# A fused recurrent attention and feed-forward block on one core: another place for the last projections of a step, and new orders on the engines beside TensorE

## The reference

```python
rkv = einsum('blh,hu->blu', inputs, W_rkv) + b_rkv
r, k, v = split(rkv, 3, axis=-1)
r, k = sigmoid(r), exp(k)
kv = k * v
# y[t] = lam * y[t-1] + u[t], along the tokens, for u = kv and u = k
u1, u2 = scan(lam, kv), scan(lam, k)
a = (u1 + gamma * kv) / (u2 + gamma * k + 1e-06) * r
x = layernorm(inputs + a @ W_o + b_o)

xr = mu_r * x + (1 - mu_r) * x_prev      # x_prev: the token before
xk = mu_k * x + (1 - mu_k) * x_prev
out = sigmoid(xr @ W_r) * (square(relu(xk @ W_k)) @ W_v)
result = layernorm(x + out)
```

## Time and profile before

| | us |
|---|---|
| median of 3 runs | 2535.43 |
| lowest and highest | 2534.3 and 2537.21 |
| the profiled execution | 2535.74 |
| its span (first to last instruction) | 2533.9 |
| TensorE busy in it | 2510.5 |
| VectorE, ScalarE, GpSimd busy | 2013.6, 1267.5, 1245.6 |

### The profile page before, as it was taken

One profiled execution on the slowest core, in us unless ns is written; L12 is line 12 of the kernel. 1 busy time (PEld: TensorE's weight loads), 2 busy tenths in 40 slices (PEclk: granted clock), 3 DMA queues, 4 the chain that ended last, 5 costly groups with the idle time before them and its releaser, 6 DMA issues.

```text
span 2533.9 us, 32904 instructions
## 1 busy us (share of the span) xinstructions
PE 2510.5 (99%) x11268; PEld 2076.7 (82%) x11268; DVE 2013.6 (79%) x2693; ACT 1267.5 (50%) x2157; POOL 1245.6 (49%) x1128
## 2 busy tenths in 40 slices
PE   7999999999999999999999999999999999999998
PEld 6888888888888888888888888888888888888877
DVE  7877888778787787887788777878777888787885
ACT  4545455444554444554545544455444555454545
POOL 6654454445454544535445444444444453545545
PEclk8999999999999999999999999999999999999999
DMA  4001110111100111111111011111111111110100
GB/s 170 26 34 51 45 39 34 34 51 50 34 34 34 51 51 34 46 38 35 51 39 45 34 35 50 50 34 34 35 50 50 34 43 34 43 51 34 51 25 34
DMA packets 57784, 110.63 MB, mean 44 GB/s; under 512 B 7040, under 2 KB 7040, under 8 KB 57088
## 3 DMA queue, kind: packets, MB, share of 16 engines
q1 hardware_dynamic: 57600, 108.31, 12.6%
HBM read 74.73 MB, written 33.55 MB: 43 GB/s over the span
## 4 chain that ended last, share of the span: by engine, by line
PE 98%; ACT 1%; POOL 0%; DVE 0%; DMA 0%; issue 0%; POOLq 0%; SPq 0%; DVEq 0%; ACTq 0%
PE bankA L1086 14%; PE bankA L1088 14%; PE bankA L1087 14%; PE bankB L1102 14%; PE bankB L1104 13%; PE bankB L1103 13%; PE bankB L1147 4%; PE bankB L1148 4%; PE bankB L1146 4%; PE bankB L1124 2%; PE bankA L1102 0%; PE bankA L1104 0%; PE bankA L1103 0%; POOL x_lo L408 0%; DMA wrkv_f<-in_w_rkv 0%; PE bankA L1148 0%
## 5 line engine op out<-in xcount | busy, mean ns | idle before, releaser
L1086 PE MATMUL bankA<-x_hi,wrkv_hi 128*128 128x512 f32 x1488 | 583.9, 392 | 4.7 <-POOL x_lo L408 4.7
L1088 PE MATMUL bankA<-x_hi,wrkv_lo 128*128 128x512 f32 x1488 | 580.5, 390 | 0.0
L1087 PE MATMUL bankA<-x_lo,wrkv_hi 128*128 128x512 f32 x1488 | 580.4, 390 | 0.0
L882 DVE RECIPROCAL gate<-gate 128x512 f32<-128x512 f32 x128 | 429.2, 3353 | 4.4
L413 POOL TENSOR_TENSOR att_f<-att_f,gate 128x512 f32<-128x512 f32 x128 | 209.4, 1636 | 280.1 <-DVE att_f L895 280.1
L1086 PEld LDWEIGHTS bankA<-x_hi,wrkv_hi 128*128 128x128 f32 x1488 | 280.3, 188 | 63.8 <-POOL x_lo L408 5.8
L1088 PEld LDWEIGHTS bankA<-x_hi,wrkv_lo 128*128 128x128 f32 x1488 | 280.1, 188 | 58.7
L1087 PEld LDWEIGHTS bankA<-x_lo,wrkv_hi 128*128 128x128 f32 x1488 | 280.4, 188 | 57.2
L424 POOL TENSOR_TENSOR ve<-mv,eps_ln 128x2 f32<-128x2 f32 x128 | 66.4, 519 | 462.6 <-DVE mv L907 459.6
L440 POOL TENSOR_TENSOR xk_lo<-xk_f,xk_hi 128x512 fp32r<-128x512 f32 x124 | 169.4, 1397 | 244.9 <-ACT xk_hi L667 244.9
L445 POOL TENSOR_TENSOR xr_lo<-xr_f,xr_hi 128x1024 fp32r<-128x1024 f32 x63 | 176.4, 2800 | 202.7 <-ACT xr_hi L672 202.7
(11 more groups left out here) (150 smaller groups left out, 5588.5 us busy)
## 6 DMA issues: line engine op xcount, KB each, us to landing
y<-in_x SPq DMA_DIRECT2D x128, 256.0 KB, 2.7
x_f<-in_xT SPq DMA_DIRECT2D x124, 256.0 KB, 4.0
out<-z SPq DMA_DIRECT2D x124, 256.0 KB, 2.1
wrkv_f<-in_w_rkv SPq DMA_DIRECT2D x3, 768.0 KB, 7.7
xk_f<-in_xT SPq DMA_DIRECT2D x4, 256.0 KB, 4.5
wo_f<-in_w_o SPq DMA_DIRECT2D x1, 1024.0 KB, 11.2
wk_f<-in_w_k SPq DMA_DIRECT2D x1, 1024.0 KB, 13.1
wr_f<-in_w_r SPq DMA_DIRECT2D x1, 1024.0 KB, 15.2
```

The costliest lines, as they stand in the source:

```text
L882: dve.reciprocal(gate[:, c % 2], gate[:, c % 2]).then_inc(rec_made, 1)
L1086: pe.matmul(bank[:], w_hi, hi[:, h], start=(h == 0), stop=False)
L1087: pe.matmul(bank[:], w_hi, lo[:, h], start=False, stop=False)
L1088: last = pe.matmul(bank[:], w_lo, hi[:, h], start=False, stop=(h == NC - 1))
```

## The change

On TensorE, within a step, the projections number (2,1), (3,1) and (3,2) are each issued one place earlier among the work of the older block: project(2,1) ahead of the transposes, project(3,1) ahead of the keys, and project(3,2) ahead of the first half of the receptance, so that between the two halves of the receptance only the first half of the values is left. Nothing is added or taken away. The other three engines get a new order for the same work.

The core of the diff:

```diff
 GpSimd, step
                 att(s, 1)
-                att_low(s, 0)
                 mixed_gate_low(s1, 0)
                 if s1.first():
                     weight_low(W_V, 3)
+                att_low(s, 0)
+                att_low(s, 1)
                 att(s, 2)
                 mixed_gate_low(s1, 1)
-                att_low(s, 1)
                 residual(s1, 0)
 ScalarE, step
                 exp_key(s, 0)
+                exp_gate(s, 0)
                 exp_key(s, 1)
-                exp_gate(s, 0)
                 if s2.exists():
                     normalise_result(s2, 1)
                 normalise_sum(s1, 0)
+                exp_gate(s, 1)
                 normalise_sum(s1, 1)
-                exp_gate(s, 1)
+                exp_key(s, 2)
                 copy_zT(s1)
                 previous_keys(s1)
                 mixed_keys_high(s1)
-                exp_key(s, 2)
                 exp_gate(s, 2)
                 previous_gate(s1, 0)
                 mixed_gate_high(s1, 0)
+                exp_key(s, 3)
                 att_high(s, 0)
-                exp_key(s, 3)
+                att_high(s, 1)
...
                 previous_gate(s1, 1)
-                exp_gate(s, 3)
                 mixed_gate_high(s1, 1)
                 tanh(s1, 0)
-                att_high(s, 1)
-                att_high(s, 2)
+                exp_gate(s, 3)
                 x_high(s.back(-1), 0)
                 x_high(s.back(-1), 1)
                 x_high(s.back(-1), 2)
+                att_high(s, 2)
                 x_high(s.back(-1), 3)
+                normalise_result(s1, 0)
+                tanh(s1, 1)
                 last_column(s1)
-                tanh(s1, 1)
-                normalise_result(s1, 0)
                 att_high(s, 3)
 VectorE, step
+                begin_sum(s1, 0)
                 if s2.exists():
                     gated_values(s2, 1)
-                begin_sum(s1, 0)
                 begin_sum(s1, 1)
-                denominator(s, 0)
                 if s2.exists():
                     statistics(s2, 1, 1, result_rows, y2_made)
+                denominator(s, 0)
...
                 denominator(s, 1)
+                numerator(s, 1)
                 mix_keys(s1)
                 mix_gate(s1, 0)
-                numerator(s, 1)
                 denominator(s, 2)
...
                 gated_values(s1, 0)
+                x_low(s.back(-1), 0)
                 statistics(s1, 1, 0, result_rows, y2_made)
-                x_low(s.back(-1), 0)
                 x_low(s.back(-1), 1)
 TensorE, step
                 project(s, 2, 0)
+                project(s, 2, 1)
                 transposes(s1)
-                project(s, 2, 1)
                 project(s, 2, 2)
                 project(s, 3, 0)
+                project(s, 3, 1)
                 keys(s1)
-                project(s, 3, 1)
+                project(s, 3, 2)
                 receptance(s1, 0)
-                project(s, 3, 2)
                 values(s1, 0)
                 receptance(s1, 1)
                 values(s1, 1)
```

## The result

The changed kernel takes 2555.73 us (median of 4 runs, 2554.55 to 2556.59), the kernel before 2534.86 (4 runs, 2533.66 to 2537.21). The ratio is 1.0081, with a 95% interval from 1.0063 to 1.0098: slower by 0.8%. The forecast was 2557, with a range of 2552 to 2573. The profiled execution of the changed kernel took 2556.59 us, 20.85 more than that of before; its span is 2554.8, 20.9 more than the 2533.9 of the earlier trace rows.

A forecast was written before the change was run, and what follows sets the result against it. TensorE bounds the kernel; `xr_lo` 0.59 us late plus 0.24 start loses 0.83 per step against 0.11 before, so 0.72 over 30 steps adds 21.6 to 2535.74, giving 2557.3 us, range 2552 to 2573.

The forecast's parts named there:

- The bound and the place: TensorE, busy 2510.5 of 2533.9 us, bounds; the loss is a wait for `xr_lo` before the second receptance half.
- the signs named beforehand: In the profile: 30 `xr_lo` waits of 0.7 to 0.9 us, about 22 us more idle, 78.8 us step, chain through L445, L672, L644, L935.
- The chain from E: From the end of the receptance's first half (E), refill, mix, `xr_hi` and subtraction make `xr_lo` at E + 5.87, due E + 5.28.
- The subtraction: GpSimd's L445 making `xr_lo` takes 2.40 us, chosen with 2.37 the shortest and 2.81 as the other end.
- Rival 1: GpSimd's subtraction is disturbed by VectorE's L879 and stays at 2.81 us: 12.3 us more, 2569.6 us; chance 0.15.
- The start behind the release: TensorE, standing idle before the second receptance half, starts 0.24 us behind `xr_lo`, against 0.16 when barely waiting; 0.83 lost per step.
- The values: First half of the values, 0.3 us late for VectorE's L941, costs nothing on top, being part of the 0.83.
- Rival 2: Second half of the values, or next block's `x_lo`, makes TensorE wait; gated tile's margin some 0.25 us; 2566 to 2587; chance 0.14.
- The other moves: Transposes, keys, moved projections, numerator and `att_low` in their new places together cost 0, bounds -1 and +3 us.
- Rivals 3 and 4: 3: chain of 5.28 us or less removes the 0.11 stall, 2532.4 us, chance 0.05; 4: pauses lower TensorE's clock, 2600 or more, 0.02.

The follow-up runs named there:

- experiment 3: Changed kernel with GpSimd's `xr_lo` made in four one-chunk instructions and TensorE waiting for each chunk where first needed: 2541.51 us, ratio 1.0025.
- experiment 4: Changed kernel with ScalarE's two tanh of the first half put ahead of the copy `xr_hi` of the second half: 2562.95 us (one run).
- experiment 2: Kernel before with only project(3,2) moved ahead of the first half of the receptance, all other engines in old order: 2595.91 us (one run).
- experiment 8: Changed kernel with `xr_lo` in four pieces awaited singly, and the values waiting for each chunk of VectorE's L941: 2534.29 us, ratio 0.9998 to before.
- experiment 7: Changed kernel with GpSimd's att_low(s, 1) put back right behind the second `xr_lo` instead of ahead of it: 2576.41 us (one run).
- Experiment 5: Changed kernel with TensorE's whole step in its old order, the other three engines keeping their new orders: 2551.41 us, ratio 1.0065.
- experiment 1: Changed kernel with project(3,2) put back between the first half of the receptance and the first half of the values: 2562.89 us, ratio 1.0110.
- experiment 6: Kernel before with ScalarE's gate exponential of chunk 3 put behind the copy `xr_hi` of the second half: 2531.04 us, ratio 0.9984 to before.

## Why the prediction was right, and where it was not

**The bound and the place.** Right. TensorE has no slack, no instruction was added, and the loss is standing still at the seam between values and second receptance. Experiment 3 takes that wait away and 14 us with it; experiment 4 lengthens its chain by 0.30 and pays for all of it. Of the signs named beforehand, the step of 78.8 us and the chain through L445, L672, L935 and L644 are there; the waits are shorter than the 0.7 to 0.9 us foreseen (0.6 at most in the steps, as the weight load's wait), and the page shows 8.6 us more idle time and not 22, because a part of each stop counts as busy.

**The chain from E.** Right to 0.04 us: mix ended at E + 2.33 (forecast 2.32), `xr_hi` at 3.42 (3.40), GpSimd started at 3.50 (3.47), `xr_lo` made at 5.91 (5.87), 30 times.

**The subtraction.** Right: 2.41 us where 2.40 was chosen between 2.37 and 2.81. Rival 1 is dead for the reason given against it: ScalarE's L612 makes the gate ready at 1071.40, long after GpSimd has begun at 1069.26, and L879 starts at 1072.25, behind the end of L445 at 1071.67. The neighbouring statement, that L445 would be 2.8 in every second instance, was wrong. With the new orders the first halves meet no longer either; GpSimd's L445, all instances, with shortest, median and longest in ns:

```profile
L445 POOL TENSOR_TENSOR xr_lo<-xr_f,xr_hi x63: 2371/2403/2415, 105.4 to 2518.7; 128x1024 fp32r<-128x1024 f32 x63
```

**The start behind the release.** This term was mis-sized. The forecast took the 0.24 of the earlier trace rows, where TensorE had long stood idle (the rows themselves give 0.15 + 0.08 = 0.23), and got 0.83 lost per step; 0.79 was measured, 1.2 us less in 30 steps. The matmul starts 0.05 behind the end of GpSimd, the second one 0.10 late, and that makes 0.16, the value of the wait that is barely one in the earlier trace rows. But the forecast's reason for choosing between the two, how long TensorE has stood, does not hold: in experiment 2 it is idle for 1.07 us at this place, about as long as the 1.12 of the earlier trace rows, and still starts 0.05 behind (1087.81 against 1087.76) and 0.10 late at the second; before the values it is idle for only 0.12 us (1065.88 less 1065.76) and starts 0.15 behind L941 (which ends at 1065.73) and 0.08 late at the second. What decides between 0.16 and 0.23 stays open. Against the profiled execution the forecast is 2557.3 to 2556.59: 1.2 us too much by this term, 0.5 too little for the thousandths behind the stops and the stretch ahead of the first keys. The other 0.9 down to the median is how far both profiled executions lie above their medians.

**The values.** "The 0.3 is part of the 0.83" is right: experiment 3 has the same 0.283 before the values, and TensorE's total in the changed kernel is set by `xr_lo` alone. But "costs nothing on top" hides that it is a limit of its own. Taking `xr_lo` away brings 0.425 and not the 0.68 that the change cost, and only experiment 8, which takes both, gets back to the time of before. Two lateness terms in series show as one until the second is removed.

**Rival 2.** Its sum was right and it did not decide: L875 ended 0.55 behind GpSimd, the first gated tile was there at 1076.25 + 0.63 = 1076.88, and TensorE wanted its bank at 1077.30, with the weight load 0.23 ahead, a margin of 0.2. Experiment 7 uses that margin up with one GpSimd instruction and loses 0.70 us per step, so it was a near thing, as the sum had said.

**The other moves at 0.** Right for the changed kernel (0.3 us lies ahead of the first keys, none in the finale). But it was right only for the orders together. Experiment 5 has the same orders on the other three engines under TensorE's old order and loses 0.63 per step at two places that never waited before. The forecast said as much for the numerator ("since the transposes come 2.72 us later"), and did not price the rest. The bank of the keys, freed by L700, was in no part of the prediction; it costs 1.02 per step when no projection stands behind the keys (experiment 1).

**Rivals 3 and 4.** The chain was 5.9 us and not 5.28. Nothing shows a stop lowering TensorE's clock: over one step of the changed kernel the granted clock (third column from the end) is 1.00, and over the whole profiled execution it is 0.996, as before.

```profile
1000.00:1078.80 78.80, 78.54 (x354) 64.67 (x353) 66.75 (x86) 38.74 (x67) 36.97 (x35) 1.00 0.12 41
```

## What to carry to other kernels

Where one engine is saturated, a reordering is priced by one subtraction for each of its inputs: the time at which it is due under the new order less the time at which its chain delivers it, per step, and only the positive ones count. A stop moves all that is due behind it, so a later input whose chain does not hang on that stop absorbs it, as `xr_lo` does the values' here. Work that looks movable is the cover of some chain; before moving it, name all the chains that it covers (here the refill of `xr_f` and also the bank freed by `Relu`), and look first for what can be shortened in the chain instead: one ScalarE instruction pair moved behind the copy gave 2 us of slack and the only gain of this study. Orders of several engines belong to each other, so a part of such a change, tried alone, says little about the whole: project(3,2) alone was 40 us slower than the whole change (experiment 2), and one line of ScalarE's order alone was faster than both kernels (experiment 6).

## What the runs showed of the hardware

A VectorE instruction of 128x512 with two inputs in SBUF that comes to a running GpSimd instruction ended 0.55 us behind it at each of these places, wherever in it it started. L875, 0.75 us alone, takes 2.26 in the changed kernel (ends at 1072.22, GpSimd at 1071.67) and 2.80 in experiment 2 (1088.31 and 1087.76); L879, 0.69 alone, takes 1.68 beside `att_low` (1090.02 and 1089.46). For half the elements it is half of that: an L935 of 128x256, 0.48 us alone, ends 0.28 behind GpSimd's L413 in the changed kernel (1128.32 and 1128.04). A VectorE instruction with one of its inputs in PSUM, the L966 at 1076.25 with GpSimd's L458 beside it from 1076.95, keeps its 1.22 for two. GpSimd, being first, keeps its 2.40 for `xr_lo`; the `att_low` right behind, which comes while L875 waits, takes 1.75 where 1.29 is its undisturbed time. That second meeting reaches far: one GpSimd instruction that nobody on TensorE's path waits for costs 0.70 us per step (experiment 7). The scan's last 0.02 us at GpSimd's start (1069.28 against 1069.26) cost nothing in 30 steps. The Trainium skill ("SBUF — State Buffer", section "SBUF: two separate sides") calls this an exclusive lock for the whole instruction; the trace agrees as far as the one that comes second is pushed behind the first, and the measured 0.55 us from GpSimd's end to VectorE's is the number that these runs give for it; it is less than the 0.69 and 0.75 us that the pushed instructions take alone.

Cutting one GpSimd instruction in four loses that protection: VectorE gets in between the pieces, and 2.40 us become 3.73 (experiments 3 and 8). The first pieces come earlier and the last one 1.3 us later, so the cut pays only where the consumer reaches the last piece late enough.
